# Three-part second layers for pairs 16 to 23 in batches 0 to 2 as well, with GpSimd subtracting the low parts

## What is computed

```python
def _expert_apply(xf, w1, b1, w2, b2):
    return jnp.maximum(xf @ w1 + b1, 0.0) @ w2 + b2
# 2 shared experts (mean), 32 routed experts of hidden size 176, top 6 of 32 by softmax gates
shared_out = sum(_expert_apply(flat, sw1[e], sb1[e], sw2[e], sb2[e]) for e in range(2)) / 2
routed_out = sum(gates[:, e:e+1] * _expert_apply(flat, rw1[e], rb1[e], rw2[e], rb2[e]) for e in range(32))
```

## Time and profile before

| | us |
|---|---|
| median of three runs | 418.9 |
| profiled execution, its own time | 418.02 |
| span of that execution | 416.2 |
| busy in the span: PE, DVE, ACT, POOL | 374.5, 307.5, 214.8, 119.2 |
| mean granted TensorE clock, share of full speed | 0.955 |

### The profile page before, as it was taken

How to read it: one execution, slowest core, us unless ns; L and a number is a source line. 1 busy time by engine, 2 the same in 40 slices (tenths; PEclk the granted TensorE clock), 3 DMA queues, 4 the chain that set the end, 5 groups by cost and what they waited for, 6 DMA issues and landing times.

```text
span 416.2 us, 7115 instructions
## 1 busy us (share of the span) xinstructions
PE 374.5 (90%) x2383; PEld 334.5 (80%) x2383; DVE 307.5 (74%) x527; ACT 214.8 (52%) x478; POOL 119.2 (29%) x88
## 2 busy tenths in 40 slices
PE   4555668579999999989999999999999999999996
PEld 3334456468899998878999988888999989999996
DVE  3499997689899955899899666998995634444443
ACT  3777534456544436546543437555432335666672
POOL 0555442003333300023334000133432003535442
PEclk8659889869999999999999999999999999999999
DMA  7343460034686321546764222576753226767520
GB/s 229 90 139 104 109 220 25 5 127 146 204 225 178 110 63 52 180 136 205 236 187 123 75 71 81 161 205 204 204 179 97 58 71 223 238 192 217 166 72 27
DMA packets 37456, 58.62 MB, mean 141 GB/s; under 512 B 5778, under 2 KB 15284, under 8 KB 37428
## 3 DMA queue, kind: packets, MB, share of 16 engines
q1 hardware_dynamic: 37428, 58.27, 46.6%
HBM read 57.06 MB, written 1.18 MB: 140 GB/s over the span
## 4 chain that ended last, share of the span: by engine, by line
PE 76%; DVE 15%; issue 6%; ACT 1%; DVEq 1%; ACTq 0%
PE acc L491 34%; PE z L510 10%; PE z L511 9%; PE z L512 9%; DVE bu L728 5%; DVE bu L721 3%; PE z L425 2%; PE acc L391 2%; PE bb L406 1%; PE cc L415 1%; PE acc L496 1%; DVE stage L822 1%; PE misc L452 1%; PE cc L440 1%; PE bb L433 1%
## 5 line engine op out<-in xcount | busy, mean ns | idle before, releaser
L643 ACT ACTIVATE z<-z,par 128x256 f32<-128x256 f32 x188 | 76.3, 443 | 137.3 <-PE z L512 137.3
L491 PE MATMUL acc<-stage,w 128*128 128x256 f32 x564 | 134.8, 382 | 0.0
L510 PE MATMUL z<-xh,w1l 128*128 128x256 f32 (+1 forms) x376 | 120.2, 320 | 0.0
L491 PEld LDWEIGHTS acc<-stage,w 128*128 128x128 f32 x564 | 102.8, 191 | 12.2
L873 POOL TENSOR_TENSOR ya<-ya,pr 128x512 f32<-128x512 f32 x42 | 54.9, 1307 | 187.9 <-DVE pr L739 187.9
L512 PE MATMUL z<-xh,w1h 128*128 128x256 f32 (+1 forms) x376 | 107.1, 285 | 0.0
L511 PE MATMUL z<-xl,w1h 128*128 128x256 f32 (+1 forms) x376 | 107.0, 285 | 0.0
L728 DVE TENSOR_TENSOR_SCAN bu<-dA,bu 128x512 f32<-128x512 f32 x64 | 78.7, 1240 | 1.7
L510 PEld LDWEIGHTS z<-xh,w1l 128*128 128x128 f32 x376 | 72.0, 191 | 4.9 <-issue 3.1
L511 PEld LDWEIGHTS z<-xl,w1h 128*128 128x128 f32 x376 | 72.0, 191 | 1.6
L512 PEld LDWEIGHTS z<-xh,w1h 128*128 128x128 f32 x376 | 72.0, 191 | 0.0
(11 more groups left out here) (113 smaller groups left out, 390.6 us busy)
## 6 DMA issues: line engine op xcount, KB each, us to landing
w<-in_w SPq DMA_DIRECT2D x92, 256.0 KB, 3.3
gone<-gates SPq DMA_DIRECT2D x64, 256.0 KB, 3.8
stage<-in_w SPq DMA_DIRECT2D x11, 512.0 KB, 3.6
grem<-gates SPq DMA_DIRECT2D x96, 48.0 KB, 3.1
xr<-in_xr SPq DMA_DIRECT2D x4, 256.0 KB, 4.2
x<-in_xT SPq DMA_DIRECT2D x4, 256.0 KB, 3.9
grem<-gates SPq DMA_DIRECT2D x32, 32.0 KB, 2.7
out<-x SPq DMA_DIRECT2D x4, 256.0 KB, 3.8
```

The lines of the kernel that those rows point to most:

```text
L491: mm = pe.matmul(acc[:, k, :], weights, h, start=t + k + n == 0, stop=last, skip_group_check=True)
L510: pe.matmul(z[p % ZB][:, i, :], w1l[:, t, one], xh_, start=k == 0, stop=False)
L643: ins = act.activation(z[p % ZB][:, i, :], z[p % ZB][:, i, :], ACT.Relu, bias=b1[:, t:t + 1])
```

## The change

`SPLIT` becomes the list 16 to 23, so the second layers of these pairs take the three-part form in batches 0 to 2 too. For those, the subtraction that makes `hl` is done by GpSimd, behind its subtraction for `w2l`, and signalled by a new semaphore `pool_hl_done`. The last batch keeps DVE's `lower_h`.

```diff
-SPLIT = []
+SPLIT = [16, 17, 18, 19, 20, 21, 22, 23]
...
+        def last(b):
+            return type(b) is int and b == B - 1
...
                 if split(b, p):
-                    pe.wait_ge(S["hl_done"], nth_split(b, p))
+                    if last(b):
+                        pe.wait_ge(S["hl_done"], p + 1)
+                    else:
+                        pe.wait_ge(S["pool_hl_done"], nth_split(b, p))
                     pe.wait_ge(S["w2l_done"], nth_split(b, p))
...
-                if exists(b, p, 1) and split(*before(b, p, 1)):
-                    lower_h(*before(b, p, 1))
+                if last(b) and p:
+                    lower_h(b, p - 1)
...
                     pool.wait_ge(S["w2h_done"], nth_split(b, p))
                     pool.tensor_tensor(w2l[:, p % 4, 0:n, :], w2[:, p % RING, 0:n, :],
                                        w2h[:, p % 4, 0:n, :].bitcast(F32), ALU.subtract).then_inc(S["w2l_done"], 1)
+                if not (type(b) is int and b == 0 and p == 0):
+                    d, q = before(b, p, 1)
+                    if q in SPLIT and not last(d):
+                        n = len(PAIRS[q])
+                        pool.wait_ge(S["hh_done"], nth_split(d, q))
+                        pool.tensor_tensor(hl[:, q % SKEW, 0:n], hg[:, q % 4, 0:n], hh[:, q % SKEW, 0:n].bitcast(F32),
+                                           ALU.subtract).then_inc(S["pool_hl_done"], 1)
```

More of the change, by code:

```diff
@@ L220, in xattn_ffn_kernel @@
                  "z_ready", "relu_done", "hg_done", "ot_done", "stored", "spilled", "lnvar_done", "aggr_done", "rs1_done", "nb1_done",
-                 "cv0_done", "y_added", "uclip_done", "usig_done", "hh_done", "hl_done", "w2h_done", "w2l_done",
+                 "cv0_done", "y_added", "uclip_done", "usig_done", "hh_done", "hl_done", "pool_hl_done", "w2h_done", "w2l_done",
                  "l2_done", "ones_done"]
@@ L489, in second_layer @@
                         for n, (weights, h) in enumerate(parts):
-                            last = p == NP - 1 and i + 1 == len(PAIRS[p]) and n + 1 == len(parts)
-                            mm = pe.matmul(acc[:, k, :], weights, h, start=t + k + n == 0, stop=last,
+                            end = p == NP - 1 and i + 1 == len(PAIRS[p]) and n + 1 == len(parts)
+                            mm = pe.matmul(acc[:, k, :], weights, h, start=t + k + n == 0, stop=end,
                                            skip_group_check=True)
```

## The result

The changed kernel took 438.5 us (median of four runs, 438.19 to 443.71) against 420.1 for the kernel before beside it: a ratio of 1.047, 95% interval 1.037 to 1.056. It is 18 us slower; 430 was forecast, in a range of 416 to 441. Two of the four runs of the kernel before were its longer ones (421.3 and 422.2); in the experiments its median was 418.3 to 418.6 in 17 and 19 runs, and against that the loss is 20 us. The profiled execution took 438.5 us with a span of 436.7, 20.5 us more than the span of before.

The account below looks back on a forecast made before the run. PE was taken to bound the tails, level with DVE in pairs 3 to 16. Stalls less PE's saving gave 4.6 + 4.6 + 2.5 = 11.7 us on 418.0: 429.7, said as 430, range 416 to 441.

Parts of the forecast that it names:

- Bound and place: PE sets the tails (pairs 17 to 23), where the change acts; in pairs 3 to 16 nothing changes.
- The turns: In the tails, DVE and POOL alternate by whole instructions where both read SBUF; DVE ends 0.55 us behind POOL.
- The second rival: POOL keeps its turn, so DVE waits for both subtractions: 11.7 us more, 441.4 us; chance 0.13.
- x1: Chain step PE needs for `mean`, early in each tail; DVE held by POOL: PE stall of 2.1 us.
- var: Tail step through L776, held by `w2l` of pair 19: PE stall of 1.4 us, 1.3 in batch 2.
- dt: Tail step of batches 0 and 1; `dtl` comes 1.05 us later, PE 0.3 sooner: stall of 0.6 us.
- turn: PE's wait for the gates late in each tail; gates 2.3 us later: stall of 1.6 us.
- ACT and the loads at no cost: ACT has room for its 1.05 us of copies per pair; earlier waits for `w2` loads costed at nothing.
- PE's saving: Three-part second layers save PE 0.31 us each in the tails: 1.5 us in batches 0 and 1, 2.5 in batch 2.
- Batch 2: Its tail: 5.0 us of stalls less eight second layers (2.5 us), so 2.5 us slower.
- third: Rival: ACT becomes the bound in pairs 22 and 23; without the port 417 to 419 us, no change; chance 0.10.
- the first rival: Not slower: POOL's subtractions fall between DVE's instructions or cost PE nothing, 414.5 us; chance 0.12.

Follow-up runs that it names:

- e1: Changed kernel with GpSimd's two subtractions left out in batches 0 to 2, PE's and ACT's work kept: 418.0 us, ratio 0.998 to the kernel before.
- e2: Changed kernel with GpSimd filling the low parts by six memsets, only a two-element subtraction reading SBUF: 419.0 us, ratio 1.001 to the kernel before.
- e5: Changed kernel with idle bf16 matmuls in PE's gaps ahead of mean, dt and, in batch 2, turn: 434.3 us, ratio 1.034 to the kernel before.
- e3: Changed kernel with all copies, subtractions and waits, but plain fp32 second layers in batches 0 to 2: 437.1 us, ratio 1.048 to the kernel before.

## Why the prediction was right, and where its sizes were off

The way (slower) and the cause were forecast. The size was not: in the traces the forecast loss was 11.7 us and the measured one 20.5, so 438.5 lies near the upper end of the range, and above the forecast's own range of 423 to 436.

**Bound and place.** Right. All of the loss is in the tails, none in pairs 3 to 16. One sign failed: POOL was to be busy for near 9 tenths of the tail, and was for 19.8 of 34 us in batch 1 and 22.2 of 30 in batch 2.

**The turns.** Right, and shown by e1, e2 and the ends of the instructions. The second rival, POOL keeping its turn, did not happen where both stood waiting: the second L773 ran between `w2l` 17, which ended at 238.92, and `hl` 16, which the trace starts at 238.89 and which ended 1.13 us behind L773. But the turn goes by instruction, not by work done, and that costs more with small ones. Batch 2's gates show it (DVE, then POOL):

```profile
353.06 1.26 DVE L810 TENSOR_TENSOR mask<-rep,lg 128x64 f32<-128x64 f32 x1
354.36 1.21 DVE L812 TENSOR_TENSOR em<-ex,mask 128x64 f32<-128x64 f32 x1
...
356.05 2.25 DVE L816 TENSOR_SCALAR g<-em,rsm 128x32 f32<-128x32 f32 x2
```
```profile
352.96 1.28 POOL L896 TENSOR_TENSOR w2l<-w,w2h 128x512 fp32r<-128x512 f32 x1 [1.03 <-ACT w2h L656]
354.19 1.29 POOL L903 TENSOR_TENSOR hl<-stage,hh 128x512 fp32r<-128x512 f32 x1
355.79 1.26 POOL L896 TENSOR_TENSOR w2l<-w,w2h 128x512 fp32r<-128x512 f32 x1 [0.30 <-ACT w2h L656]
357.01 1.26 POOL L903 TENSOR_TENSOR hl<-stage,hh 128x512 fp32r<-128x512 f32 x1
```

Four DVE instructions that take 0.2 us each waited for one POOL instruction each. L816 has one input tensor in SBUF, as has L700: the forecast cited that the Trainium skill's page "SBUF — State Buffer", section "SBUF: two separate sides", counts such fast-mode instructions in, and left them out of its sum for want of a row. They were held as well, and the trace agrees with the page. On L816 alone this costs 1.9 us in the gates.

**The stalls,** forecast against PE's waits in batch 1: x1 2.1, measured 2.3; var 1.4, measured 1.0; dt 0.6, measured 0.7; turn 1.6, measured 0.3. The last is short because PE itself came late there, at half clock: in e5, at full clock, it is 1.4. In batch 2 they are 2.1, 1.0 and 3.2 against 2.1, 1.3 and 1.6: the turn was mis-sized by half, for the small instructions just shown.

**ACT and the loads at no cost.** Right but for dt: e1 keeps both and costs nothing. The 1.05 us showed as the 0.7 us at L448 (L445 before) in each of batches 0 and 1.

**PE's saving** was mis-sized: "less five second layers (1.5)" twice and "less eight second layers (2.5)", 5.5 us in all. Part of it the sum gave back itself, since its stalls were counted with PE arriving sooner (0.31 at var, 0.3 at dt, 0.6 at turn). Without any saving the same steps give about 4.9 us in batches 0 and 1 and 4.1 in batch 2, so the saving was worth some 2.2 us of the sum, most of it in batch 2. By e3 and e5 it was worth nothing. Even without POOL's work, e1 gained 0 and 0.2 us in batches 0 and 1, where 0.6 each was forecast, and 2.3 in batch 2, where 2.2 was.

**Batch 2** was mis-sized most. At full clock, in e5, the tails are 5.1, 5.1 and 5.0 us longer than before, against 4.6, 4.6 and 2.5 forecast. The turn's 3.2 us in place of 1.6 is the larger part of that difference of 2.5; the rest isn't taken apart.

**Not foreseen:** the clock after a stall, 4 to 5 us by e5. The forecast priced each gap at its own length. With the 3.5 us just named this makes up the difference of 8.6 us between the forecast tails (11.7) and the measured ones (20.3).

**The rivals.** As an account of the loss, ACT as the bound (third) falls with e1. But its figure for a change without the port, 417 to 419 us, is where e1 and e2 landed (418.0 and 419.0), and the first rival's 414.5 is not. In e1 ACT is busy for 6.89 of the 7 us from 250 to 257, pairs 22 and 23 of batch 1, against 4.97 before, and relu of pair 23 begins at 254.98 instead of 253.50 (e1's batch 1 runs 0.3 us late as a whole).

**What stays open:** why e1 gains next to nothing in the tails of batches 0 and 1. Its trace shows where the gain goes: in batch 1 PE is 0.5 us ahead at turn and 1.1 us by the end of pair 2's first layer, and then waits 0.5 us for DVE's `bu` (0.8 in batch 0), which the kernel before does not. This fits the forecast's remark that DVE is level with PE from pair 0 on, but no run tells whether the full ACT or DVE's own work makes `bu` late. Nor was it tried what decides whether the clock falls: the gap of 2.35 us ahead of `mean` in batch 0 (148.79) was followed by no stretch at half clock, the same gap in batch 1 was; the wait of 0.65 us at `dt` was followed by one in the changed kernel and in e2, and not in e1.

## What to carry to other kernels

Before an idle GpSimd is given elementwise work, look at what VectorE does at that time: here its instructions with two SBUF inputs, and fast one-input ones, alternated with GpSimd's by whole instructions, and short ones in a dependent chain lost most for their size. Idle time of an engine isn't free capacity if its work takes turns with the critical chain. And a saving on the engine that sets the pace was worth nothing from the moment that a side effect made another chain set it: price the side effect first, then ask what is left of the saving.

## What the runs showed of the hardware

- Six memsets and a two-element subtraction on GpSimd, 1.0 us together, left VectorE's two-input instructions at 692 ns; one 128 x 512 subtraction with two SBUF inputs stretched them to 1.4 us on average (L777, L782).
- A VectorE multiply of 128 x 64 elements took 1.21 us instead of 0.22 when it had to let a GpSimd instruction pass; a fast one-input instruction of 128 x 512 took 1.49 instead of 0.42.
- After a gap of 2.3 us the TensorE clock was at 1.2 GHz for 3.4 us, though the matmuls had been back to back again from its first microsecond; with bf16 matmuls in the gaps it stayed at 2.4 GHz. A gap of the same length in another batch was not followed by a fall.
